# A two-layer token tower: projection in half precision, one piece per slot, ids in small transfers, another order at the start

## The reference

```python
embed = table[y]                       # table: 256 x 128
x = conv(pad(embed), conv_w)           # two taps, 16 groups
out = relu(x) @ proj_w.T + proj_b      # 64 features

pre = inp @ W_ih.T + (b_ih + b_hh)     # twice, 256 states
h = tanh(p_t + h @ W_hh.T)             # 1024 steps, one after the other

h = tok(x)
h = h + rnn2(layernorm(h)) @ fc_w.T + fc_b
h = h + select_ffn(layernorm(h))
h = h + phasor_attention(layernorm(h))
h = h + experts(layernorm(h))          # 8 experts, the best 2 of each token
```

## Time and profile before

| | us |
|---|---|
| median of 3 runs | 1386.47 |
| lowest and highest | 1385.34, 1390.23 |
| profiled execution | 1385.33 |
| its span, first to last instruction | 1383.5 |
| first recurrent state (ScalarE) | 50.34 |
| last subtraction of the recurrence (VectorE) | 896.61 |

### The profile page before, as it was taken

How to read it: one execution, slowest core, us unless ns; L and a number is a source line. 1 busy time by engine, 2 the same in 40 slices (tenths; PEclk the granted TensorE clock), 3 DMA queues, 4 the chain that set the end, 5 groups by cost and what they waited for, 6 DMA issues and landing times.

```text
span 1383.5 us, 64463 instructions
## 1 busy us (share of the span) xinstructions
PE 1209.8 (87%) x27009; PEld 998.9 (72%) x27009; DVE 814.0 (59%) x3407; ACT 828.9 (60%) x4697; POOL 108.8 (8%) x162
## 2 busy tenths in 40 slices
PE   2599999998999999999999999884666884799998
PEld 1499999998999998999999999822225873233332
DVE  5555565665565565556556555456782554677775
ACT  1366666666666666666666766563557661456554
POOL 2300000000000000000000000000110111111010
PEclk9555555555555555555555555587777996899999
DMA  5001000000001000000000000000000000000000
GB/s 153 6 4 20 4 4 19 5 5 19 4 5 20 5 4 19 5 4 5 4 5 4 4 5 4 4 16 1 0 0 0 1 0 0 1 15 8 15 8 15
DMA packets 21563, 14.52 MB, mean 10 GB/s; under 512 B 10737, under 2 KB 20529, under 8 KB 21297
## 3 DMA queue, kind: packets, MB, share of 16 engines
q1 hardware_dynamic: 21296, 10.69, 3.5%
HBM read 8.55 MB, written 2.13 MB: 8 GB/s over the span
## 4 chain that ended last, share of the span: by engine, by line
PE 62%; issue 32%; DVE 2%; POOL 2%; DMA 1%; ACT 0%; POOLq 0%; SPq 0%; DVEq 0%; ACTq 0%
PE bank L577 38%; PE bank L666 6%; PE bank L652 4%; PE bank L429 3%; PE bank L437 2%; PE bank L508 2%; PE bank L647 2%; POOL stat L322 1%; PE bank L661 1%; PE bank L1366 1%; PE bank L383 1%; PE bank L1180 1%; DMA space<-in_x 1%; PE bank L1376 0%; DVE space L696 0%
## 5 line engine op out<-in xcount | busy, mean ns | idle before, releaser
L577 PE MATMUL bank<-space,whh_hi 128*128 128x8 f16 x16384 | 614.9, 170 | 13.8 <-issue 7.8
L577 PEld LDWEIGHTS bank<-space,whh_hi 128*128 128x128 f16 x16384 | 550.3, 106 | 38.0 <-issue 8.1
L696 DVE TENSOR_TENSOR space<-h_f,space 128x16 f16<-128x16 f32 x2048 | 356.5, 176 | 359.4 <-ACT h_f L677 317.1
L677 ACT ACTIVATE h_f<-bank 128x16 f32<-128x16 f32 x2048 | 377.8, 184 | 274.7 <-PE bank L577 262.6
L683 ACT ACTIVATE space<-bank 128x16 f16<-128x16 f32 x2048 | 376.8, 184 | 11.4 <-PE bank L577 11.4
L666 PE MATMUL bank<-space,wih_hi 128*128 128x32 f16 x2048 | 178.3, 188 | 2.6 <-issue 2.6
L577 PE MATMUL bank<-space,whh_lo 128*128 128x32 f16 (+2 forms) x2192 | 147.6, 189 | 0.0
L429 PE MATMUL bank<-onehot,tab 128*128 128x128 f16 x448 | 120.0, 268 | 4.8 <-DVE onehot L414 4.8
L652 PE MATMUL bank<-xr,wih_lo 128*128 128x32 f16 x512 | 123.4, 241 | 0.0
L1180 PE MATMUL bank<-xt,wx 128*128 (+1 forms) x352 | 110.0, 407 | 11.0 <-ACT xt L334 11.0
L666 PEld LDWEIGHTS bank<-space,wih_hi 128*128 128x128 f16 x2048 | 114.2, 104 | 2.7 <-issue 2.7
(11 more groups left out here) (252 smaller groups left out, 1672.3 us busy)
## 6 DMA issues: line engine op xcount, KB each, us to landing
space<-in_x SPq DMA_DIRECT2D x7, 516.0 KB, 9.0
out<-res SPq DMA_DIRECT2D x8, 256.0 KB, 2.6
space<-in_wrec SPq DMA_DIRECT2D x1, 768.0 KB, 9.8
space<-in_wx SPq DMA_DIRECT2D x1, 740.5 KB, 11.6
space<-in_x SPq DMA_DIRECT2D x1, 512.0 KB, 9.9
brec<-in_brec SPq DMA_DIRECT2D x1, 512.0 KB, 4.5
space<-router_dram SPq DMA_DIRECT2D x8, 64.0 KB, 2.3
ew<-in_ew SPq DMA_DIRECT2D x1, 256.0 KB, 3.9
```

What stands on the lines that cost most here:

```text
L577: mm = pe.matmul(own[:, m, :], w[:, k, m * P:(m + 1) * P], steps(h, k), start=False, stop=False, skip_group_check=True)
L677: act.activation(h_f[layer][:, s % 2, :, :], own, ACT.Tanh, scale=scale[layer]).then_inc(s_h[layer], 1)
L696: dve.tensor_tensor(h[layer][:, :, s % RINGS[layer], 1, :], h_f[layer][:, s % 2, :, :], h[layer][:, :, s % RINGS[layer], 0, :], ALU.subtra ...
```

## The change

- The projection's operands are split: `relu` and `wproj` into high and low half-precision parts, three matmuls (high x high, high x low, low x high) for one in fp32. ScalarE writes the rectified high part, VectorE the low (`rectified_low`). `wproj` gets a scale of its own, from the same all-reduce as the tables'.
- LEAD is 33 and the pieces have other numbers o: one-hot matmuls at 4 to 11 and 14 to 21, projection two matmuls in each of 24 to 26, transposes at 44 and 77, output matmuls one in a slot (two at 60), router columns at 79 and 80. The first slots, which hold only pieces, are laid into the start of each engine (`lead_in`).
- Layer 0's ring is 128.
- The first tile's ids are loaded first of all; the others come in 28 transfers, one for each piece, four buffers.
- In the norms the division by 64 goes into the subtraction and into ScalarE's scale; epsilon is added by GpSimd ahead of the root.
- At the start only whh of layer 0 and wih of layer 0 are split before the first tile's norm, the other recurrent weights behind it, the wide weights' maxima and splits in the slots of periods 1 and 2. GpSimd handles the biases on 65 partitions, splits them between the first and the second all-reduce, and scales them afterwards.

```diff
-RINGS = (32, 256)
+RINGS = (128, 256)
...
-PERIOD, LEAD = 32, 6
+PERIOD, LEAD = 32, 33
+ROWS = 65
...
+            [(vid[:, :], a["vid"]), (embt[:, :], a["embt"]), (wconv[:, :, :], a["wconv"]), (wproj[:, :], a["wproj"])],
+            [(brec[0:ROWS, :, :].rearrange("p a h -> p (a h)"), a["brec"].partition_broadcast(ROWS)),
+             (bsum[0:ROWS, B_O:B_O + 2 * D], a["bov"].partition_broadcast(ROWS))],
-             (wproj[:, :], a["wproj"]), (bproj[:, :], a["proj_b"].partition_broadcast(P)),
...
-             (brec[:, :, :].rearrange("p a h -> p (a h)"), a["brec"].partition_broadcast(P)),
...
-            link(dve.tensor_scalar(r.stat[:, 1, :], r.stat[:, 0, :], 1.0 / D, None, ALU.mult))
         def centre(dve, r, g):
-            dve.tensor_tensor(r.xc[:, :, :], r.cur[:, :, :], r.each(1), ALU.subtract).then_inc(g.centred, 1)
+            dve.scalar_tensor_tensor(r.xc[:, :, :], r.each(0), -1.0 / D, r.cur[:, :, :], ALU.mult,
+                                     ALU.add).then_inc(g.centred, 1)
...
-        def variance(dve, link, r, g, k):
+            act.activation(r.sq[:, :, :], r.xc[:, :, :], ACT.Square, scale=D ** -0.5).then_inc(g.squared, 1)
+        def variance(dve, r, g, k):
             dve.wait_ge(g.squared, k + 1)
-            link(dve.reduce_sum(r.stat[:, 2, :], r.sq[:, :, :], AX.X))
-            dve.tensor_scalar(r.stat[:, 3, :], r.stat[:, 2, :], 1.0 / D, EPS, ALU.mult, ALU.add).then_inc(g.variance, 1)
-        def root(pool, r, g, k):
...
+        def root(pool, link, r, g, k):
             pool.wait_ge(g.variance, k + 1)
+            link(pool.tensor_scalar(r.stat[:, 3, :], r.stat[:, 2, :], EPS, None, ALU.add))
...
-            if 4 <= o < 20:
-                b, n = (o - 4) // 8, (o - 4) % 8
+            if 4 <= o < 12 or 14 <= o < 22:
+                b, n = (o - 4) // 10, (o - 4) % 10
                 v, tap, part = n // 4, n // 2 % 2, n % 2
                 if o == 4:
                     pe.wait_ge(s_oh, m + 2)
+                elif o == 14 and m:
                     pe.wait_ge(prep.copied, m + 2)
                 mm = pe.matmul(P_CONV[:, b * P:(b + 1) * P], tab[part][:, v, tap, :],
                                onehot[:, m % 2, v, b, tap:tap + P], start=(n == 0), stop=(n == 7),
                                skip_group_check=True)
-                if o == 19:
+                if o == 21:
                     mm.then_inc(s_conv, 1)
-            elif o in (22, 23):
-                b = o - 22
-                pe.wait_ge(s_relu, 2 * m + 4)
-                mm = pe.matmul(P_PROJ[:, b * D:(b + 1) * D], relu[:, b, :], wproj[:, :], start=True, stop=True,
-                               skip_group_check=True)
-                if b == 1:
+            elif 24 <= o < 27:
+                pe.wait_ge(s_relo, m + 3)
+                for c in (2 * (o - 24), 2 * (o - 24) + 1):
+                    mm = project(pe, P_PROJ, [x[:, c // 3, :] for x in relu], c // 3, c % 3)
+                if o == 26:
                     mm.then_inc(s_proj, 1)
-            elif o == 33:
+            elif o == 44:
...
+        def project(pe, own, x, b, c):
+            part, w = ((0, 0), (0, 1), (1, 0))[c]
+            return pe.matmul(own[:, b * D:(b + 1) * D], x[part], wproj16[w][:, :], start=(c == 0), stop=(c == 2),
+                             skip_group_check=True)
...
+        def rectified_low(dve, low, conv, high):
+            dve.scalar_tensor_tensor(low, conv, 0.0, high, ALU.max, ALU.subtract).then_inc(s_relo, 1)
...
-            if 24 <= o < 30:
-                if o == 24:
+            turns = (54, 55, 59, 60, 60, 61, 62, 63, 64, 65, 66, 67)
+            if o in turns:
+                if o == turns[0]:
                     pe.wait_ge(s_lo[1], OPEN + (j + 1) * UNIT)
-                for c in (2 * (o - 24), 2 * (o - 24) + 1):
+                for c in range(turns.index(o), turns.index(o) + turns.count(o)):
                     mm = output(pe, O_SUM, c // 6, j, b0 + c // 6, c % 6)
-                if o == 29:
+                if o == turns[-1]:
                     mm.then_inc(s_fc, 1)
-            elif o == 43:
+            elif o == 77:
...
+            if 16 <= o < 20:
+                one_hot(dve, k + 1, o - 16)
+            if k == 1 and 0 <= o < 12:
+                wide_most(dve, link, o)
+            elif k == 1 and o == 20:
+                scales(dve, link, S_FF1, S_END, 3, 0)
+            elif k == 2 and o < 20 and o % 10 != 5:
+                wide_weights(dve, link, o - (o > 5) - (o > 15))
...
+            if k == 1 and o == 14:
+                pool.wait_ge(s_mx, 3)
+                pool.partition_all_reduce(stat[:, 6, 0:6], most[:, 0:6], P, RMAX).then_inc(s_mxa, 1)
+            if k == 1 and o == 24:
+                pool.wait_ge(s_prep, 4)
+                own = bias[0:ROWS, B_V:B_V + D]
+                pool.tensor_tensor(own, own, scl[0:ROWS, S_V:S_V + 1].to_broadcast([ROWS, D]), ALU.mult).then_inc(s_wide, 1)
+            if o == 31 and 0 <= k < SUBS:
+                root(pool, link, prep_room, prep, k + 2)
+            if o == 72 - 2 * PERIOD and 0 <= k - 6 < SUBS:
+                root(pool, link, done_room, done, k - 6)
...
-            for g in range(-PERIOD // 2 - 2, T + OFF + LATE):
+            for g in range(-9, T + OFF + LATE + 2):
...
+            def some_ids(sp, m):
+                j, b0 = place(m + 4)
+                sp.dma_start(ids[:, m % 4, :, :],
+                             a["x"][b0:b0 + 2, j * UNIT - 1:(j + 1) * UNIT].partition_broadcast(P)).then_inc(
+                                 s_ids[m % 4], 16)
+            sp.dma_start(ids0[:, :, 1:UNIT + 1], a["x"][:, 0:UNIT].partition_broadcast(P)).then_inc(s_ids0, 16)
+            for g in range(4):
                 for dst, src in loads[g]:
                     sp.dma_start(dst, src).then_inc(s_w[g], 16)
...
-            for j in range(2, T // UNIT):
-                sp.wait_ge(s_oh, 4 * (j - 2) + 1)
-                sp.dma_start(ids[:, j % 2, :, :],
-                             a["x"][:, j * UNIT - 1:(j + 1) * UNIT].partition_broadcast(P)).then_inc(s_ids[j % 2], 16)
+                if g == 2:
+                    for m in range(4):
+                        some_ids(sp, m)
+            for m in range(4, SUBS):
+                sp.wait_ge(s_oh, m - 2)
+                some_ids(sp, m)
...
+            link = Chain(pool, pool_chain)
+            def split_rows(a, z):
+                for part in range(3):
+                    link(pool.tensor_copy(bpart[0:ROWS, a:z], bsum[0:ROWS, a:z]))
+                    link(pool.tensor_copy(bias[32 * part:32 * part + 1, a:z], bpart[32 * part:32 * part + 1, a:z]))
+                    if part < 2:
+                        link(pool.tensor_tensor(bsum[0:ROWS, a:z], bsum[0:ROWS, a:z], bpart[0:ROWS, a:z], ALU.subtract))
+            pool.wait_ge(s_w[1], 16 * len(loads[1]))
+            for l in range(2):
+                link(pool.tensor_tensor(bsum[0:ROWS, l * H:(l + 1) * H], brec[0:ROWS, 2 * l, :],
+                                        brec[0:ROWS, 2 * l + 1, :], ALU.add))
             pool.wait_ge(s_mx, 1)
-            pool.partition_all_reduce(stat[:, 6, 3:4], stat[:, 5, 3:4], P, RMAX).then_inc(s_mxa, 1)
+            pool.partition_all_reduce(stat[:, 6, 3:5], stat[:, 5, 3:5], P, RMAX).then_inc(s_mxa, 1)
+            split_rows(0, 2 * H + 2 * D)
             pool.wait_ge(s_mx, 2)
             pool.partition_all_reduce(stat[:, 6, 0:3], stat[:, 5, 0:3], P, RMAX).then_inc(s_mxa, 1)
-            link = Chain(pool, pool_chain)
...
-            pool.wait_ge(s_w[1], 16 * len(loads[1]))
             pool.wait_ge(s_prep, 2)
             for l in range(2):
-                own = bsum[:, l * H:(l + 1) * H]
-                link(pool.tensor_tensor(own, brec[:, 2 * l, :], brec[:, 2 * l + 1, :], ALU.add))
-                scaled(own, l)
-            split_rows(0, 2 * H)
-            pool.tensor_copy(stat[:, 6, 7:8], stat[:, 6, 0:1]).then_inc(s_bias, 1)
+                own = bias[0:ROWS, l * H:(l + 1) * H]
+                pool.tensor_tensor(own, own, scl[0:ROWS, l:l + 1].to_broadcast([ROWS, H]), ALU.mult).then_inc(s_bias, 1)
             for i, r in enumerate(halves_of):
-                root(pool, r, prep, i)
+                root(pool, link, r, prep, i)
...
+            slot = lambda e, g: rec_scalar(e, g, rescale)
+            lead_in(act, slot, -17, -12)
+            halves_scalar(act, prep, 0, xr[:, :, 0:UNIT], (bank[4], bank[5]), 0,
+                          lambda: lead_in(act, slot, -12, -9))
+            recurrence(act, slot)
...
+            lead_in(pe, rec_tensor, -45, -9)
...
+            for i in range(2):
+                dve.wait_ge(s_relu, i + 1)
...
+                rectified_low(dve, flat[1], bank[i][:, :], flat[0])
+            def split(hi, lo, w, s):
+                link(dve.tensor_scalar(hi, w, scl[:, s:s + 1], None, ALU.mult))
+                return dve.scalar_tensor_tensor(lo, w, scl[:, s:s + 1], hi, ALU.mult, ALU.subtract)
```

(26 more changed lines are left out.)

228 lines of the change are left out of this document (105 added, 123 removed).

## The result

| | before | after |
|---|---|---|
| median, us | 1385.9 (4 runs) | 1363.12 (4 runs) |
| lowest, highest | 1384.82, 1390.23 | 1362.05, 1367.79 |
| profiled execution, its span | 1385.33, 1383.5 | 1363.57, 1361.6 |
| first recurrent state | 50.34 | 64.49 |
| state of slot 22 | 67.04 | 82.08 |

The account below looks back on a forecast made before the run. Bound by the recurrence's latency loop per slot, plus TensorE running out of instructions: 1385.3 - 39.8 (recurrence) + 10.3 (start) - 0.1 (tail) = 1355.7 us; own range 1349 to 1362, 8-in-10 range 1346 to 1368.

Parts of the forecast that it names:

- rival (b): TensorE's instruction queue: small id transfers starve it as the large did, byte for byte; +11, 1366.7 us; chance 0.12.
- The slot price: Recurrence: each slot costs the larger of latency loop (0.753 us) and TensorE's sum; full period 24.87, 1001 slots 778.0 us.
- the 1.3 us of waiting: Recurrence: TensorE's waiting kept in the forecast beside small id transfers, the small waits that had no transfer near.
- its 0.55: Recurrence: cost in us of five tiny linked instructions at once, for the wide weights' scales, within a 1.1 us term.
- Ids: Token ids in small transfers: TensorE's stands of about 12 us together in the recurrence shrink to 1.3 us.
- 0 and all of 12: Recurrence: bounds in us for TensorE's waiting that remains with small id transfers; 1.3 was taken.
- The start: Before the recurrence: four GpSimd switches between all-reduces and elementwise work in a row on the path; net +10.3 us.
- the switch to elementwise: GpSimd at the start: the change from all-reduce to elementwise instructions takes 7.3 us, bounds 7.2 to 8.1.
- the bound of +14 for the start: Before the recurrence: upper bound in us of the start's net loss, forecast +10.3; lower bound +6 with short switches.
- Rival (a): GpSimd at the start: switches cost nothing because loads proceed while it waits; -5.6 instead of +10.3, 1339.8 us; chance 0.10.
- The end: Tail behind the recurrence: shorter norms drop two chain steps of 0.17 and add one on GpSimd; -0.1 us.
- Rival (c): Recurrence: no slack when every slot is filled, 0.827 us a slot; 46 us more, 1402 us; chance 0.04.

Follow-up runs that it names:

- the three edits taken back: Changed kernel with one edit undone in each, one run each: fp32 projection 1383.02 us; output matmuls in pairs 1368.07 us; layer 0's ring of 32 steps 1362.73 us.

## Why the prediction was right, and where it was off

The total is right by a margin that owes something to luck. 1363.12 lies above the 1349 to 1362 that the forecast gave itself, and inside 1346 to 1368 only because that range was drawn wide enough for rival (b). It is nearer to (b)'s 1366.7 than to 1355.7, and yet (b) is not what happened: no stand is left on TensorE. The recurrence came out as worked out, the start is what was off.

**The slot price: right.** A slot is the larger of a latency loop and TensorE's sum, and with that 1001 slots came to 778.05 where 778.0 stood. The parts are less exact, and that they meet so closely is luck: the period is 0.07 dearer (24.94 for 24.87, some 2 us over the recurrence), and the 1.3 us of waiting that were kept for the small transfers didn't come. The period with the wide weights' splits (slots 31 to 63, 89.03 to 114.43) takes 25.40 and the next one 24.57, so these cost 0.83; the slot with the five linked scales (1.19 long) lies ahead of slot 22, in the start, though its 0.55 was counted here.

What the 39.7 us are made of, from the runs that take one edit back or make one alone: projection 19.8, ids 12.7, single output matmuls 5.2, the ring nothing. That would leave 2.0 for the other positions, such as transposes that no longer share a slot with a one-hot matmul. But the ids' part isn't one number: put back into the changed kernel, the large transfers cost 16.8 us, and with that the parts come to more than the whole. So the 2.0 is not shown.

**Ids: right,** in both directions. Of the bounds "0 and all of 12" for what would remain, the lower one was met. Rival (b) is refuted. The rule that stood beside it, of the Trainium skill, "Runtime: NRT & Kernel Launch", section "Instruction fetch mechanics", that crossing a block of instructions is mostly hidden, holds here with small transfers and not beside large ones (5.11 us at one crossing).

**The start: the mechanism right, one term mis-sized.** The step that was off is "I take 7.3 for the switch to elementwise and 5.7 for the switch to the all-reduce (bounds 7.2 to 8.1, and 4.6 to 5.9)". The other three took 6.93, 5.80 and 6.98. The first took 10.87, with its time falling on the weight transfers; with these held back it took 5.73. The bounds came from the changes in the kernel before. One of these, back to elementwise work, did lie beside loads and took only 8.08; but that trace holds no change to the all-reduce beside the loads whose length could be read, because its first one (12.5 us of idle ahead of 15.23) had nothing to show where its work began. The Trainium skill, "GPSIMD Engine Reference", section "Instruction dispatch", has about 6 us for the first call to a freshly loaded kernel. If a change of kind is such a call, the trace agrees with the size in quiet (5.73 to the all-reduce; back it is 6.93) and shows that it is paid at every change, and nearly twice that beside some loads. With the page's figure the forecast of the start would have been further off.

The first all-reduce was forecast at 20 and came at 25.79; the 5.8 us went through to the second all-reduce (forecast 40.7, measured 46.62), and 4.7 of them to the first states (forecast 59.8, measured 64.49). Even the bound of +14 for the start was passed, by 1.0. Rival (a), changes that cost nothing, is refuted by the same chain, and by the 15.9 us that the old order gives back.

**The end: -0.1 was forecast and +2.8 measured, most of it probably scatter.** Behind slot 1023 this kernel took 501.47, the one before 498.67. Up to GpSimd's clearing of `cp`, 22.5 us on, the two differ by 0.1. Later the same 95 matmuls, 13 VectorE and 21 ScalarE instructions took 24.3 us before and 25.7 after, and another 1.3 comes in the stretch behind. Windows view, before and then after:

```profile
1047.10:1071.40 24.30, 14.38 (x95) 14.27 (x96) 5.55 (x13) 19.37 (x21) 0.00 (x0) 0.72 0.00 1
```

```profile
1022.50:1048.20 25.70, 15.70 (x95) 15.59 (x96) 5.55 (x13) 19.29 (x21) 0.00 (x0) 0.67 0.00 1
```

The granted clock (second to last but one column) is 0.72 and 0.67: the step between its two levels, 1.2 and 2.4 GHz, falls elsewhere. One row of sixteen fp32 matmuls, before and then after:

```profile
1065.41 2.54 PE L1290 MATMUL bank<-space 128*128 128x128 f32 x16
```

```profile
1040.75 3.62 PE L1357 MATMUL bank<-space 128*128 128x128 f32 x16
```

Over the eleven profiles, with the same code there, this last stretch takes 498.7 to 502.7: 498.7 and 500.4 with the old recurrence ahead of it, 499.6 to 502.7 with the new one (500.5 in the middle). The profile of before was the shortest of all. That the new program makes it longer by a little can't be excluded from two profiles against nine. The spread of 4 us is larger than the 2.9, so I put most of the 2.9 down to it.

**Rival (c)**, slots that cost 0.827 when all are filled, is refuted: a full period takes 24.94, or 0.78 a slot, and slots filled with projection or single output matmuls take 0.75 to 0.76.

So 1355.7 + 4.7 (first change) + 0.0 + 2.9 (end) = 1363.3 against the profiled 1363.57.

## What to carry to other kernels

Count an engine's changes between kinds of work as instructions: list them in program order, and put all work of one kind together. Here twelve instructions in another order cost 16 us, and replacing the two reductions by two small matmuls each bought 5 more. Where an engine stands with nothing to wait for, look at what the DMA queues do in that time: a price read in a quiet stretch need not hold beside transfers, and a large transfer may cost elsewhere than where its data is used. And pieces of side work should be laid out by what a slot has left: two short matmuls were free there, and two fp32 ones cost 0.35 each.

## What the hardware showed that I had not expected

Where the DMA engines were idle, or busy for at most 0.27 of the time, GpSimd's change from elementwise work to an all-reduce took 5.7 to 6.2 us and the change back 6.9 to 7.6, but for one of 10.91 (0.25, the large ids). With more transfers beside it, it took 10.2 to 11.0 in seven cases: to the all-reduce 10.87, 11.02 (large ids), 10.38, 10.74 and 11.01 (the three edits taken back), and back 10.17 and 10.67. In three other cases, all of the change back, it took only 7.36, 7.79 (small ids in the kernel before) and 8.08, though the DMA engines were busy for 0.56 to 0.79 of the time. Casts and copies ran without one: after the all-reduce at 25.79 a cast starts at 26.05.

The stands of TensorE behind a large transfer and the longer changes of GpSimd look like one thing, code that comes late because the DMA engines are busy. For TensorE the profile shows it: no block of its instructions moves while the 516 KB transfer runs (none from 312.4 to 322.9, ids from 315.8 to 323.0), and work goes on when one has landed. For GpSimd the long changes hold no instruction block in any queue, and the three shorter ones beside heavy loads speak against so simple a cause, so that part is argued and not shown.

Six of VectorE's ten small instructions took 0.54 to 0.77 us instead of 0.16 to 0.28 while GpSimd was working (15.7 to 22.8 us in the kernel with matmuls for the maxima). From 22.8 to 28.5 us, with GpSimd idle and the DMA engines still busy for 0.51 of the time, the small ones took 0.16 to 0.29 again, so the transfers alone don't do it. In a start that is VectorE's own chain I put the 1.5 us over the expectation down to it; no run separates it.
